# A turned value product with a bias maximum in the first layer, and the last batch's sums and feed-forward in another order

## The reference

```python
# layer 0: 16 heads of 16, the first 100 rows of the context are seen at most (causal)
scores = jnp.where(causal, jnp.einsum('bhqd,bhkd->bhqk', qh, kh) * inv_sqrt_d, lowest)
attn = jax.nn.softmax(scores, axis=-1)
x = x + jnp.einsum('bhqk,bhkd->bhqd', attn, vh).reshape(b, sq, H) @ Wout.T
x = x + moe(_layernorm(x))            # top-1 of 8 experts plus a shared expert
# layer 1: 16 heads over 1444 rows of the context, latent products, then a ternary feed-forward
x = x + (softmax(q_r @ k_r.T) @ kv_r) @ w_kc_kv.T @ Wo.T
h = rms_norm(silu(bit_linear(xn, w_gate)) * bit_linear(xn, w_up), ln_weight)
x = x + bit_linear(h, w_down)         # bit_linear quantises its input by its largest magnitude
```

## Time and profile before

| What | Value |
|---|---|
| Time, median of 3 runs (lowest, highest) | 1025.56 us (1021.11, 1026.66) |
| The profiled execution, its span | 1029.42 us, 1027.7 us |
| Mean granted clock of TensorE | 0.909 |
| Busy PE, DVE, POOL, ACT | 888.6, 586.8, 477.5, 397.3 us |
| GpSimd's subtraction of the maximum (L630) | 8 of 2860 ns mean |
| GpSimd's additions to acc (L569) | 160 of 1918 ns mean |
| GpSimd's power for the norm of h (L591) | 0.55 us for batch 6 |
| One Exp of 16 heads (L1393) | 8 of 1536 ns mean |

### The profile page before, as it was taken

How to read it: one execution, slowest core, us unless ns; L and a number is a source line. 1 busy time by engine, 2 the same in 40 slices (tenths; PEclk the granted TensorE clock), 3 DMA queues, 4 the chain that set the end, 5 groups by cost and what they waited for, 6 DMA issues and landing times.

```text
span 1027.7 us, 15558 instructions
## 1 busy us (share of the span) xinstructions
PE 888.6 (86%) x5880; PEld 666.7 (65%) x5880; DVE 586.8 (57%) x1102; ACT 397.3 (39%) x801; POOL 477.5 (46%) x478
## 2 busy tenths in 40 slices
PE   4996777788899877999988989989889889899974
PEld 3584666656798755777766767667667667665532
DVE  3214555242223655666758857857866865964645
ACT  2322222221122213545455455355355355345442
POOL 3002222127000502787677676666666566456760
PEclk9956878789899978999999999999999899999996
DMA  9207000226985100000000000000001000000000
GB/s 206 83 1 245 2 1 1 58 84 216 323 292 204 33 17 15 1 10 24 1 24 10 1 17 21 1 9 29 1 9 29 1 9 13 1 10 6 8 12 9
DMA packets 42150, 52.27 MB, mean 51 GB/s; under 512 B 12214, under 2 KB 35688, under 8 KB 41820
## 3 DMA queue, kind: packets, MB, share of 16 engines
q1 hardware_dynamic: 41052, 49.63, 15.6%
q0 software_dynamic: 1024, 1.64, 0.5%
HBM read 45.80 MB, written 5.36 MB: 50 GB/s over the span
## 4 chain that ended last, share of the span: by engine, by line
PE 65%; DVE 15%; DMA 6%; ACT 5%; issue 5%; POOL 2%; SPq 0%; POOLq 0%; ACTq 0%; DVEq 0%
PE ps L1125 12%; PE ps L1137 9%; PE ps L1105 6%; PE ps L1049 5%; PE ps L973 4%; PE ps L1160 3%; PE ps L1076 3%; DVE nm L1827 2%; PE ps L1054 2%; PE ps L986 2%; DMA xs<-xs_scratch 2%; PE ps L784 2%; PE ps L811 2%; PE ps L862 2%; PE ps L847 1%
## 5 line engine op out<-in xcount | busy, mean ns | idle before, releaser
L569 POOL TENSOR_TENSOR acc<-acc,pt 120x800 f32<-120x800 f32 (+1 forms) x160 | 306.9, 1918 | 126.0 <-ACT pt L1556 93.2
L1556 ACT ACTIVATE pt<-ps 120x400 f32<-120x400 f32 (+1 forms) x384 | 189.5, 504 | 237.3 <-PE ps L1125 230.0
L1827 DVE TENSOR_REDUCE nm<-ps 128x1 f32<-128x482 f32 (+1 forms) x336 | 215.9, 655 | 109.6 <-PE ps L1105 107.2
L1125 PE MATMUL ps<-qh,khl 128*120 128x400 f32 (+1 forms) x384 | 167.9, 437 | 24.9 <-ACT pt L1556 24.6
L1105 PE MATMUL ps<-khl,qh 128*128 128x482 f32 (+1 forms) x336 | 136.5, 409 | 11.7 <-DVE nm L1827 10.0
L1137 PE MATMUL ps<-pt,kv 120*64 120x400 f32 (+1 forms) x768 | 141.4, 503 | 0.0
L1125 PE MATMUL ps<-ql,kh 65*120 65x400 f32 (+1 forms) x384 | 137.2, 357 | 0.0
L1125 PEld LDWEIGHTS ps<-qh,khl 128*120 128x120 f32 (+1 forms) x384 | 73.4, 191 | 72.1 <-ACT pt L1556 36.1
L1137 PEld LDWEIGHTS ps<-pt,kv 120*64 120x64 f32 (+1 forms) x768 | 51.2, 136 | 64.5 <-issue 56.4
L1049 PEld LDWEIGHTS ps<-x3T,wqb 128*128 128x128 f32 x512 | 77.3, 197 | 6.9 <-DVE xyz L1798 1.7
L1049 PE MATMUL ps<-x3T,wqb 128*128 128x100 f32 x512 | 75.7, 276 | 2.7 <-ACT x3T L1330 1.4
(11 more groups left out here) (270 smaller groups left out, 1367.7 us busy)
## 6 DMA issues: line engine op xcount, KB each, us to landing
egu<-_L_ffn_gate_up_proj_dram SPq DMA_DIRECT2D x14, 1024.0 KB, 6.2
edn<-in_L_ffn_down_proj_dram SPq DMA_DIRECT2D x14, 512.0 KB, 7.5
spread<-inv_scratch SPq DMA_DIRECT2D x30, 100.0 KB, 2.7
craw<-in_ctx_dram SPq DMA_DIRECT2D x8, 360.0 KB
wo_n<-in_L_xattn_Wo_dram SPq DMA_DIRECT2D x1, 2048.0 KB, 10.9
wq_n<-in_L_xattn_Wq_dram SPq DMA_DIRECT2D x1, 2048.0 KB, 9.7
xs_scratch<-zero SPq DMA_DIRECT2D x1, 1792.0 KB, 12.7
xs<-xs_scratch SPq DMA_DIRECT2D x14, 128.0 KB, 5.6
```

The lines of the kernel that those rows point to most:

```text
L569: nc.gpsimd.tensor_tensor(total[r, :, :], before[r, :, :], pt[j % PT_BUF][r, :, :], ALU.add).then_inc(p_added, 1)
L1125: last = mm(ps[0:key_rows(t), k % 2, 0:HT], lhs[:, keys], rhs[:, HT * a:HT * a + HT], start=first, stop=not first)
L1556: nc.scalar.activation(pt[j % PT_BUF][0:rows, k % 2, :], ps[0:rows, k % 2, 0:HT], ACT.Exp).then_inc(p_ready, 1)
L1827: nc.vector.tensor_reduce(nm3[0:w, i, n:n + 1], ps[0:w, 3 + m % 2, 0:MN], AX.X, ALU.max).then_inc(m_reduced, 1)
```

## The change

In the first layer the value product takes the turned weights as its loaded operand and the 17 used columns of the values as its streamed one, so that its output has tokens on the partitions; `vT`, its keep and its four turns are gone, and the product stands behind the turns of ao and xn. The maximum is negated and scaled on VectorE and enters 16 Exp, one per head, as their bias; GpSimd's subtraction is gone. ScalarE copies both halves of the turned weights, ahead of the Exp of the step; VectorE's residual and its statistics come first in its step, and one step later than before.

In the last batch, GpSimd leaves out the last three tiles of the last unit (`ADDED_LAST = 9`), and TensorE adds these tiles and `acc` up in one accumulation (`last_sums`). The up products of batch 6 go to banks 3 and 4 at slots 32 and 33 (from 37 and 39), the rest of its feed-forward follows from slot 33 on, and its turn of hq, keep and down product stand at slots 45, 46 and 47, within the loop, where they stood behind it. The order behind the loop becomes sums, four parts of the output product, then batch 7.

```diff
--- before.py
+++ after.py
@@ -83,11 +83,14 @@
 GU_SLOT, SILU_SLOT, HIDDEN_SLOT = (40, 41, 45), 41, (42, 46)
-LAST_GU_SLOT, LAST_SILU_SLOT, LAST_HIDDEN_SLOT = (31, 37, 39), 32, (38, 40)
+LAST_GU_SLOT, LAST_SILU_SLOT, LAST_HIDDEN_SLOT = (31, 32, 33), 32, (33, 34)
+LAST_UP_BANK = 3
 SQ_SLOT, HN_SLOT, H_NORM_SLOT = 1, 4, 3
 QH_SLOT = (13, 17, 20, 23)
-LAST_SQ_SLOT, LAST_HN_SLOT, LAST_H_NORM_SLOT = 40, 42, 42
-LAST_QH_SLOT = (44, 45, 46, 47)
+LAST_SQ_SLOT, LAST_HN_SLOT, LAST_H_NORM_SLOT = 35, 36, 36
+LAST_QH_SLOT = (38, 40, 42, 43)
+LAST_HQ_SLOT, LAST_KEEP_HQ_SLOT, LAST_DOWN_SLOT = 45, 46, 47
+ADDED_LAST = KT - 3
 HQ_SLOT, KEEP_HQ_SLOT, DOWN_SLOT, RESULT_SLOT = 30, 31, 34, 36
@@ -557,6 +558,8 @@
             u, t = j // KT, j % KT
+            if u == NU - 1 and t >= ADDED_LAST:
+                return
             pool.wait_ge(p_ready, 2 * j + 2)
@@ -621,19 +624,10 @@
             pool.wait_ge(rstd_ready, 1)
-            nc.gpsimd.memset(vaug[:, :, :, HD + 1:HS], 0.0).then_inc(vaug_set, 1)
             nc.gpsimd.memset(vaug[:, :, :, HD:HD + 1], 1.0).then_inc(vaug_set, 1)
-            for i in range(B + 2):
-                if i < B:
-
-                    pool.wait_ge(s0_max, i + 1)
-                    nc.gpsimd.tensor_tensor(sm[i % 2][:, :, :], sm[i % 2][:, :, :],
-                                            mx0[i % 2][:, :].unsqueeze(2).to_broadcast([S, NH, S]),
-                                            ALU.subtract).then_inc(s0_shifted, 1)
-                if i >= 2:
-                    b = i - 2
-                    pool.wait_ge(var2_ready, b + 1)
-                    power(rstd[:, b:b + 1], veps[:, b:b + 1], S).then_inc(rstd2_ready, 1)
+            for b in range(B):
+                pool.wait_ge(var2_ready, b + 1)
+                power(rstd[:, b:b + 1], veps[:, b:b + 1], S).then_inc(rstd2_ready, 1)
@@ -835,33 +829,21 @@
                     pe.wait_ge(s0_exp, b + 1)
+                    if b >= 2:
+                        pe.wait_ge(o0_kept, b - 1)
+                    if b >= 3:
+                        pe.wait_ge(xn2_kept, b - 2)
                     for half in range(2):
-                        if half == 1:
-                            pe.wait_ge(p0_kept_a, b + 1)
-                        elif b:
-                            pe.wait_ge(p0_kept_v, b)
-                            pe.wait_ge(ao_ready, b)
-                            if step >= 4:
-                                pe.wait_ge(xn2_kept, step - 3)
+                        if half:
+                            pe.wait_ge(p0_kept, 2 * b + 1)
                         for j in range(8):
...
                         last.then_inc(p0_turned, 1)
-                    if b:
-                        pe.wait_ge(vT_kept, b)
-
-                    if b >= 3:
-                        logits(b - 3)
                     pe.wait_ge(s0_masked, min(step + 1, B))
...
                     qb_head(2 * b + 1)
-                    pe.wait_ge(p0_kept_v, b + 1)
-                    for i in range(HG):
-                        for g in range(NG):
-                            h = HG * g + i
-                            last = mm(ps[HS * i:HS * i + HS, 6, S * g:S * g + S], vaug[:, b, h, :],
-                                      pT[:, NG * i + g, :], start=True, stop=True)
-                    last.then_inc(pv0_done, 1)
+                    pe.wait_ge(p0_kept, 2 * b + 2)
                 if 2 <= step <= B + 1:
@@ -878,7 +860,18 @@
                     last.then_inc(xn2_turned, 1)
+                if 1 <= step <= B:
+
+                    b = step - 1
+                    if b >= 3:
+                        logits(b - 3)
+                    for h in range(NH):
+                        g, i = h // HG, h % HG
+                        last = mm(ps[0:S, 6, (HD + 1) * h:(HD + 1) * h + HD + 1], pT[:, NG * i + g, :], vaug[:, b, h, 0:HD + 1],
+                                  start=True, stop=True)
+                    last.then_inc(pv0_done, 1)
                 if 2 <= step <= B + 1:
@@ -886,17 +879,9 @@
                     last.then_inc(out0_done, 1)
-                if 1 <= step <= B:
-
-                    b = step - 1
-                    pe.wait_ge(vT_kept, b + 1)
-                    for g in range(NG):
-                        last = turn(ps[0:S, 4, 128 * g:128 * g + 128], vT[:, S * g:S * g + S], ident[:, :])
-                    last.then_inc(v_turned, 1)
...
             pe.wait_ge(xn2_kept, B)
-            pe.wait_ge(vT_kept, B)
             for b in range(B - 3, B):
@@ -1188,14 +1173,16 @@
                 half = part - 1
-                if half:
+                if b == B - 2:
+                    pe.wait_ge(m_kept, NU)
+                elif half:
                     pe.wait_ge(h1_part, 2 * b + 1)
...
                 for c in range(DC):
-                    last = mm(ps[0:S, 5, :], xqT[:, c, :], wuT[:, c, 512 * half:512 * half + 512],
+                    last = mm(ps[0:S, LAST_UP_BANK + half if b == B - 2 else 5, :], xqT[:, c, :], wuT[:, c, 512 * half:512 * half + 512],
                               start=c == 0, stop=c == DC - 1)
@@ -1203,6 +1190,8 @@
                 pe.wait_ge(xq_kept, b + 2 if b < B - 2 else b + 1)
+                if b == B - 2:
+                    pe.wait_ge(y_ready, b)
                 o = ps[:, 5, :].bitcast(BF16)
@@ -1265,6 +1254,10 @@
                         gate_and_up(b - 1, ffn_slots(b, GU_SLOT, LAST_GU_SLOT).index(s))
+                    if b == B - 1 and s == LAST_HQ_SLOT:
+                        turn_hq(B - 2)
+                    if b == B - 1 and s == LAST_DOWN_SLOT:
+                        ffn_down(B - 2)
                     if u + 1 < NU and at == TURN_MAX_AT:
@@ -1307,13 +1300,21 @@
-            sum_weights(NU - 1)
-            for part in range(2):
+            def last_sums():
+
+                pe.wait_ge(p_added, (KT - 1) * (NU - 1) + ADDED_LAST - 1)
+                parts = [(key_rows(0), acc[(NU - 1) % 2])]
+                for t in range(ADDED_LAST, KT):
+                    parts.append((key_rows(t), pt[(KT * (NU - 1) + t) % PT_BUF]))
+                for n, (rows, src) in enumerate(parts):
+                    for a in range(2):
+                        last = mm(ps[CD * a:CD * a + CD, 0, 0:HT], ones[0:rows, :], src[0:rows, a, :],
+                                  start=n == 0, stop=n == len(parts) - 1)
+                last.then_inc(sums_done, 1)
+
+            last_sums()
+            for part in range(4):
                 attention_out(B - 1, part)
-            turn_hq(B - 2)
-            for part in range(2, 4):
-                attention_out(B - 1, part)
-            ffn_down(B - 2)
             turn_xq(B - 1)
@@ -1384,25 +1385,16 @@
                     b = step - 1
-                    act.wait_ge(p0_turned, 2 * b + 1)
                     if b:
                         act.wait_ge(pv0_done, b)
-                    keep(pT[:, 0:8, :].rearrange("p (a j) q -> p a (j q)", a=2), ps[0:S, 4:6, 0:HT]).then_inc(p0_kept_a, 1)
-                if step < B:
-                    act.wait_ge(s0_shifted, step + 1)
-                    nc.scalar.activation(sm[step % 2][:, :, :], sm[step % 2][:, :, :], ACT.Exp, scale=HD ** -0.5)\
-                      .then_inc(s0_exp, 1)
-                if 1 <= step <= B:
-                    h = 2 * (step - 1)
-                    act.wait_ge(qb_product, h + 1)
-                    o = ps[:, h % 4, 0:DC * QB].rearrange("p (c q) -> p c q", c=DC)
-                    keep(wqb[:, :, h, :], o[:, :, 0:128])
-                    keep(wqt[:, :, h, :], o[:, :, 128:QB]).then_inc(qb_kept_a, 1)
-                if 1 <= step <= B:
-                    act.wait_ge(pv0_done, step)
-                    if step >= 2:
-                        act.wait_ge(v_turned, step - 1)
-                    keep(vT[:, :], ps[:, 6, 0:HT]).then_inc(vT_kept, 1)
+                    for half in range(2):
+                        act.wait_ge(p0_turned, 2 * b + half + 1)
+                        keep(pT[:, 8 * half:8 * half + 8, :].rearrange("p (a j) q -> p a (j q)", a=2), ps[0:S, 4:6, 0:HT])\
+                            .then_inc(p0_kept, 1)
+                    act.wait_ge(qb_product, 2 * b + 1)
+                    o = ps[:, 2 * b % 4, 0:DC * QB].rearrange("p (c q) -> p c q", c=DC)
+                    keep(wqb[:, :, 2 * b, :], o[:, :, 0:128])
+                    keep(wqt[:, :, 2 * b, :], o[:, :, 128:QB]).then_inc(qb_kept_a, 1)
                 if 2 <= step <= B + 1:
@@ -1411,6 +1403,12 @@
                     keep(xnT[:, :, S * b:S * b + S], o).then_inc(xn2_kept, 1)
+                if step < B:
+                    act.wait_ge(s0_max, step + 1)
+                    for h in range(NH):
+                        last = nc.scalar.activation(sm[step % 2][:, h, :], sm[step % 2][:, h, :], ACT.Exp, scale=HD ** -0.5,
+                                                    bias=mx0[step % 2][:, h:h + 1])
+                    last.then_inc(s0_exp, 1)
@@ -1572,6 +1570,8 @@
                         square_h(B - 2)
```

(40 more changed lines are left out.)

11 lines of the change are left out of this document (4 added, 7 removed).

## The result

The changed kernel took 1018.44 us (median of 14 runs, 1011.35 to 1023.83) against 1026.13 us for the kernel before, measured beside it (14 runs, 1021.11 to 1033.06). The ratio is 0.9923, with a 95% interval of 0.9898 to 0.9947: faster by 0.8%, 3.4 us above the 1015.0 that was forecast, within the range and on the side forecast. A run over 1.5% above the fastest of the same kernel counts in no ratio. The profiled execution took 1016.52 us, with a span of 1014.8 us and a mean granted clock of 0.899 (0.909 before).

What follows compares the result with a forecast made beforehand. No engine fills the first layer's steps, so they can shorten until TensorE is the bound. First layer -8.9 us and last batch -1.6, together -10.5, taken from the median 1025.56 give 1015 us; forecast case 1008 to 1021, range 1000 to 1031.

Steps and rivals of the forecast that it cites:

- The step: First layer, one step per batch: TensorE's 11.36 us of work plus 0.93 of waiting, 12.29 instead of 13.73; seven steps -10.1.
- The first value product: First layer, ahead of the seven steps: 5.79 us at the low clock level instead of 3.47, +2.3.
- the drain: First layer, behind the seven steps: the keep and turns of vT leave the path, 0.51 + 0.60, -1.1 us.
- ScalarE's round: First layer, each step: 8.09 us plus 4.0 for sixteen Exp, 12.1, just under TensorE's 12.29.
- (a): Last batch: TensorE sums tiles 9 to 11 itself; the wait of 3.26 and the 0.89 become 3.56 us, -0.6.
- (b): Last batch, from the end of the sums to the residual: 4.4 us instead of 7.1, -2.7.
- (c): Last batch, slots 45 to 47: turns of hq 0.51, keep 0.84 and down product 0.89 move there, +2.2 us.
- (d): Last batch: the two up products move from slots 37 and 39 to 32 and 33, where TensorE idles, -1.5 us.
- (e): Last batch, slot 45: a new wait of the turns of hq for VectorE's quantisation, 0 to 2.6 us, taken as 1.0.
- the first rival: First layer: the clock falls, a step of 14.9 us at 1.2 GHz throughout, 1033.5 us in all; chance 0.20.
- The second: First layer: the clock stays up, a step of 9.4 us, 995.5 in all, or 1005 at half; chance 0.20.
- The fourth: Last batch: the end gives nothing, the wait for hq at 2.6 us; 1016.7 in all, within the forecast's range.

Runs made afterwards that it cites:

- first_alone: The change's first layer with the last batch of the kernel before; ratio to the kernel before 0.9857 (0.9795 to 0.9919).
- bias_alone: The kernel before with only the maximum as a bias, sixteen Exp in place of GpSimd's subtraction and one Exp; ratio 0.9986 (0.9956 to 1.0015).
- last_alone: The change's last batch with the first layer of the kernel before; ratio to the kernel before 1.0006 (0.9970 to 1.0043).
- down_behind: The changed kernel with batch 6's turns of hq, keep and down product moved behind the last sums; 1012.73 us, ratio to the kernel before 0.9834.
- first_and_sums: The change's first layer and, of its last batch, only the three tiles summed on TensorE; ratio to the kernel before 0.9845 (0.9785 to 0.9905).
- spread: The changed kernel with a query-key product between the halves of the turns and the output product between the value product's halves; ratio to before 0.9970.
- first_and_feed: The change's first layer and, of its last batch, only the feed-forward's new slots; ratio to the kernel before 0.9847 (0.9793 to 0.9900).

## Why the prediction was right, and where it was not

The sign and the size came out, 1018.4 against 1015.0, but by terms that missed in opposite directions, and that they nearly cancel is luck. Summed by stretches of the profiled executions: first layer -12.5 us (forecast -8.9), last batch +2.55 (forecast -1.6), together -9.9 (forecast -10.5). The sign of the last batch was wrong.

- **The step: right in size, not in its parts.** Forecast 11.36 of work and 0.93 of waiting; measured 11.26 busy, and 0.99 between the halves: 12.24 against 12.29, and 7 steps gave -10.4. The value product was 3.06 in the mean of seven (forecast 3.15), near its lower end. But the 10.80 that the forecast starts from was one window of 14.0 us; the mean of the seven steps was 10.23 of work and 3.49 of waiting. So the work rose by 1.03 where I had 0.56, and the waiting fell by 2.50 where I had 2.00: two misses that cancel, luck again. The clock fell from 0.79 over the same stretch of before to 0.68, and the work behind the value product became dearer (the output product by 0.90), the query-key products cheaper (2.41 for 2.91). These I had carried over at their old lengths.
- **The first value product: wrong, +2.3.** I took the low level, 5.79 us, since the old one ran at 3.47. It took 2.92, 0.55 less than the old one. Together with the drain, -1.5 instead of -1.1 (187.27 to 199.00 against 199.58 to 212.80), this is why the first layer gave 3.6 us more, in this execution; the same code elsewhere took 3.0 us less to 3.2 more.
- **ScalarE's round: sized low, without effect.** I took 4.0 us for the sixteen Exp; the row has 4.40. The Trainium skill (ScalarE: Activation LUTs, "What ACT_TABLE_LOAD costs") gave 4.4 as an estimate, by a surcharge of about 93 ns for a bias by pointer and neighbours that overlap by as much; the trace agrees with it and not with my bound by the copies. It decided nothing: in the change TensorE waits for no Exp.
- **(a), (b): right.** The sums stand right behind the last values and take 2.9 us (forecast 3.56); from their end to the residual are 4.8 us (forecast 4.4), where 7.1 stood. The wait of 3.26 that (a) removes was a large one: first_alone and bias_alone, with the same last batch, have 1.64 and 0.17, and last values of 4.32 and 5.60 us in place of 2.91. What the values lost, that wait hid.
- **(c), (d), (e): the step that failed.** I took 1.0 us for the wait for hq, from a bound of 0 to 2.6, with nothing behind it but its own length. It was 1.40, and it came on top of a gain of 1.5, (d), that did not come: TensorE was free for the turns of hq 26.35 us after the start of the stretch, as before (26.29), since the values ahead took 4.69 instead of 2.91. Faster values would have gained nothing there, for the path goes over VectorE: GpSimd's norm ended at 969.28, behind its additions, as forecast, and VectorE then needed until 978.54, 9.2 us against 7.9 before, because the divide (L1843, 2.13 us where it took 0.56 before) now lies between. That is 2.0 us ahead of the turns. Behind them the keep cost what (c) had for it (0.75 of waiting, priced at 0.84), but the down product took 1.95 instead of 0.89 and the last values 4.62 on the chain instead of 2.91, which I had carried over at their old lengths. With the residual (+0.35), the shorter sums (-0.84) and 0.2 of small gains these are 2.0. Together they are 4.0 of the 4.15 us by which the last batch missed. That the cost goes with these slots is shown, by last_alone and down_behind. That the waits cause the low clock of the values is not: in first_and_sums, without them, the last values took 5.24 us.
- **The rivals.** The clock did fall, as the first rival said, but behind the value product and not in it: it took part of what the waits had given, and only single steps, as in first_alone (16.65 us) and spread (16.3 twice), show the whole of it. The second, the clock up, shows for two steps, 10.58 and 10.51, at 0.76, and late in other executions (10.82 at 0.91 in first_and_feed, 10.83 at 1.00 in spread); it lasted in none. The fourth, the end giving nothing, was right in size (last_alone is at 1.0006) but not by its cause: the wait was 1.40 and not 2.6.

Open: why the steps go from 10.5 to 13.6 us. In the change the fourth product (3.32) is the first with logits (L796) right ahead of it, but these four short products don't do it by themselves: in first_and_feed, whose first layer is the same, the third product takes 3.20 without them, and two later steps that have them take 11.04 and 10.82 us.

## What to carry to other kernels

When work is moved ahead into a loop to shorten a tail, price the whole chain that it brings along, each link against the slot where it now stands: in the tail it may have lain under another engine's work for nothing, as the turns and the down product do under the inversions. When an engine that waited becomes full, don't carry its old durations over: here a step lost 2.5 us of waiting and took on 1.0 us of work, with a lower clock. Take the mean of several steps as the start of a sum, not one of them. And look at the edited stretch, not at the whole time alone, where untouched stretches differ by more than the edit is worth, once several kernels have shown how much that stretch varies with equal code.

## What the runs showed of the hardware that was not expected

- The granted clock was lower where TensorE waited less: 0.79 at 75% busy (71.58 of 96.00 us), 0.68 at 92%, and 0.50 at 98% in a window of spread. At the low level the same work fills more time (the eight turns of L840 take 0.90 us in the change's second step and 1.57 in its fifth), so these shares don't tell which came first.
- A product of 100 loaded and 17 streamed columns costs 86 ns an instruction at 2.4 GHz (2.76 us for 32) and 171 to 177 ns at 1.2 GHz; the bounds of 89 and 181 ns from products with 8 streamed columns held to within 6%, so that between 8 and 17 columns the price hardly changes.
- The same instructions in the same order ran at different clocks, from step to step and from one execution to the next: in first_and_feed a step of 13.59 us at 0.63 and a later one of 10.82 at 0.91, in first_alone one of 16.65 at 0.50.
